# Down weights without row means, output as y times r plus x1, and the last two batches summed by TensorE

## What is computed

```python
x = x + _layernorm(attn(_layernorm(x)))
x = x + _layernorm(ffn(_layernorm(x)))          # the second line is what the change touches
# ffn: xf the tokens, w their weights for the two best of 8 experts
out = _swiglu(xf, sWg, sWu, sWd)                 # shared expert
for e in range(8):
    out = out + w[:, e:e+1] * _swiglu(xf, Wg[e], Wu[e], Wd[e])
# _swiglu(x, wg, wu, wd) = silu(x @ wg) * (x @ wu) @ wd ;  wd is 256x128
# _layernorm(y) = (y - mean(y)) / sqrt(var(y) + 1e-5), over the 128 columns
```

## Time and profile before

| | |
|---|---|
| three runs | 517.92, 518.85, 522.02 us (median 518.85) |
| the profiled execution | 518.35 us, span 516.6 us |
| busy in the span | PE 431.8, PEld 347.9, DVE 340.0, ACT 273.6, POOL 267.4 us |
| chain that ended last | PE 52%, DVE 25%, POOL 6%, issue 6%, DMA 5%, ACT 3% |
| instructions | 9625 |

### The profile page before, as it was taken

The page is one execution under the profiler, slowest core; times in us unless marked ns, Lnnn a source line. Parts: engine busy times, 40 slices in busy tenths (PEclk is TensorE's granted clock), DMA queues, the critical chain, the costliest instruction groups (busy, mean ns, idle before and its releaser), DMA issues.

```text
span 516.6 us, 9625 instructions
## 1 busy us (share of the span) xinstructions
PE 431.8 (84%) x2578; PEld 347.9 (67%) x2578; DVE 340.0 (66%) x1560; ACT 273.6 (53%) x629; POOL 267.4 (52%) x325
## 2 busy tenths in 40 slices
PE   5876989789799999998999999879996799989000
PEld 5645667476687878787878787765895699977000
DVE  7697797977785298539744965564372123199997
ACT  5453565566455574656456643646443254535753
POOL 4000017265475147735772677477777777766400
PEclk9997999999999999999999999999999699999655
DMA  7872001041433323451344225531664767794663
GB/s 235 274 280 82 2 6 59 29 128 58 133 103 113 113 75 97 121 158 60 98 141 134 86 76 153 147 117 60 188 209 138 213 201 204 234 417 148 221 251 122
DMA packets 41562, 73.44 MB, mean 142 GB/s; under 512 B 8771, under 2 KB 23622, under 8 KB 40486
## 3 DMA queue, kind: packets, MB, share of 16 engines
q1 hardware_dynamic: 32870, 54.07, 33.7%
q0 software_dynamic: 8640, 18.76, 10.1%
HBM read 45.41 MB, written 27.39 MB: 141 GB/s over the span
## 4 chain that ended last, share of the span: by engine, by line
PE 52%; DVE 25%; POOL 6%; issue 6%; DMA 5%; ACT 3%; SPq 2%; DVEq 0%; POOLq 0%
PE bank_h L909 7%; PE bank_g L884 7%; PE bank_h L884 6%; POOL slots_dram L655 5%; PE bank_g L892 3%; PE bank_h L892 3%; PE bank_h L919 3%; PE bank_t L813 2%; PE bank_p L884 2%; DMA slots_dram<-u_rows,slot_i 2%; PE bank_p L701 2%; DVE keep L1404 2%; DVE st_r L1290 2%; DVE keep L1886 2%; DVE hid_s L1370 2%
## 5 line engine op out<-in xcount | busy, mean ns | idle before, releaser
L655 POOL DMA_INDIRECT slots_dram<-u_rows,slot_i x128 | 123.2, 963 | 158.7 <-DVE u_rows L1542 122.2
L665 POOL DMA_INDIRECT routed_dram<-pair_rows,yi x142 | 138.3, 974 | 52.7 <-issue 36.1
L1370 DVE TENSOR_TENSOR hid_s<-act_s,bank_h 128x512 f32<-128x512 f32 x68 | 46.4, 682 | 83.7 <-PE bank_h L884 57.3
L884 PE MATMUL bank_h<-xbT,wgu_slots 128*128 128x256 f32 x224 | 59.5, 389 | 8.5 <-DVE hid_s L1370 8.5
L909 PEld LDWEIGHTS bank_h<-wdn,hid_s 128*128 128x128 f32 x408 | 54.1, 194 | 16.6 <-issue 15.0
L1139 ACT ACTIVATE pair_rows<-bank_h,yw 128x128 f32<-128x128 f32 x102 | 31.9, 364 | 62.6 <-PE bank_h L909 62.4
L884 PE MATMUL bank_g<-xbT,wgu_slots 128*128 128x256 f32 x224 | 59.1, 387 | 2.3 <-DMA wgu_slots<-wgu_dram 1.1
L909 PE MATMUL bank_h<-wdn,hid_s 128*128 x408 | 55.2, 279 | 4.0 <-DVE hid_s L1370 2.4
L1051 ACT ACTIVATE act_s<-bank_g 128x512 f32<-128x512 f32 x68 | 40.5, 595 | 26.4 <-PE bank_g L884 14.0
L884 PEld LDWEIGHTS bank_h<-xbT,wgu_slots 128*128 128x128 f32 x224 | 42.1, 192 | 18.2 <-DVE hid_s L1370 12.8
L884 PEld LDWEIGHTS bank_g<-xbT,wgu_slots 128*128 128x128 f32 x224 | 38.7, 193 | 6.8 <-issue 2.2
(11 more groups left out here) (315 smaller groups left out, 934.5 us busy)
## 6 DMA issues: line engine op xcount, KB each, us to landing
wgu_slots<-wgu_dram SPq DMA_DIRECT2D x71, 256.0 KB, 2.6
wgu_slots<-slots_dram SPq DMA_DIRECT2D x36, 144.0 KB, 2.3
xb<-slots_dram SPq DMA_DIRECT2D x35, 144.0 KB, 2.8
keep<-in_L_attn_x SPq DMA_DIRECT2D x8, 512.0 KB, 4.0
work<-routed_dram SPq DMA_DIRECT2D x4, 1024.0 KB, 7.3
out_dram<-keep SPq DMA_DIRECT2D x7, 512.0 KB, 2.6
routed_dram<-pair_rows,yi POOLq DMA_INDIRECT x142, 2.6
wgu_dram<-keep SPq DMA_DIRECT2D x2, 1024.0 KB, 7.6
```

What stands on the lines that cost most here:

```text
L655: g.indirect_dma_start(slots_dram, bass.IndirectOffsetOnAxis(ap=slot_i[k % 2][:, c * NT + t:c * NT + t + 1], axis=0), u_row[k % 2][:, t, : ...
L665: g.indirect_dma_start(routed_dram, bass.IndirectOffsetOnAxis(ap=yi[:, h % (2 * YB), at:at + 1], axis=0), yb[h % YB][:, at, :], None).then ...
L884: last = mm(bank[:, c * W:(c + 1) * W], w_unit(n)[:, which * INTER + c * P:which * INTER + (c + 1) * P], xbT[:, n % RING, :], start=True, ...
L1370: v.tensor_tensor(hid[:, k % RING, :], act_g[k % (RING if k >= PLAIN else 2)], up_bank(k)[:, :], ALU.mult).then_inc(hid_sb, 1)
```

## The change

The mean of a row of `hidden @ wd` over its 128 columns is `hidden` times the row means of `wd`. If each row of every down weight has its mean taken off once, all y have mean zero, and the norm is y*r. So:

- VectorE sums the rows of the shared expert's down weights after step 0 and of the eight experts' after step 1 and scales the sums; GpSimd subtracts them from the weights in place; TensorE waits for that before its first shared and its first expert down product.
- ScalarE adds the attention norm's shift to x1 in place, tile by tile, in stages 2 to 5 of steps 1 to 3 and in slots 5 to 11 of steps 4 to 8.
- The output is one VectorE instruction per tile, x1 = y*r + x1. ScalarE's and VectorE's normalizations and the 1024-wide residual adds go.
- Groups are (0), (1,2), (3,4); batch 5 is summed and measured by VectorE alone; batches 6 and 7 are summed by TensorE: an identity matrix times the shared output and times both rows of each pair, into two PSUM banks per batch. ScalarE squares these tiles with an accumulating output, VectorE makes r from the sums of squares and writes the output straight from PSUM.
- Batch 7 is written and stored lower half first.

```diff
-C_GROUPS = ((0, 1, 8), (1, 2, 8), (3, 2, 8), (5, 2, 6), (7, 1, 4))
+C_GROUPS = ((0, 1), (1, 2), (3, 2))
+X1_TILES = {2: range(0, 2), 3: range(2, 5), 4: range(5, 6), 5: range(6, 8)}
+X1_OF_SLOT = {5: range(0, 2), 6: range(2, 3), 7: range(3, 4), 8: range(4, 5), 9: range(5, 6), 10: range(6, 7), 11: range(7, 8)}
...
+            def centre(blocks, means, count):
+
+                pool.wait_ge(block_means, count)
+                g.tensor_tensor(blocks, blocks, means.unsqueeze(2).to_broadcast(list(blocks.shape)), ALU.subtract).then_inc(centred, 1)
+
+            centre(swdn_blocks, block_mean[:, 0:IC], 1)
+            centre(wdn_blocks, block_mean[:, IC:], 2)
             pool.wait_ge(ew_loaded, 16 * (4 + NE))
...
                 if stage in (4, 6):
+                    if first:
+                        pe.wait_ge(centred, 1)
...
+            pe.wait_ge(centred, 2)
             for s in range(MIX, PLAIN_STEP):
                 mixed(s)
...
+            def sum_routed(b):
+
+                for h in range(2):
+                    mm(sum_banks(b)[h][:, :], ident[:, :], kept(b, (NT + 4 * h) * E, (NT + 4 * h + 4) * E), start=True, stop=False)
+                for h in range(2):
+                    if b == B - 1 and h:
+                        pe.wait_ge(pair_in_2, 16)
+                    else:
+                        pe.wait_ge(pair_in[b % SLOTS_C], 16 * (b // SLOTS_C + 1))
+                    for c in range(2):
+                        last = mm(sum_banks(b)[h][:, :].rearrange("p (t n) -> p t n", n=E), ident[:, :], pair(b)[:, 4 * h:4 * h + 4, c, :], start=False, stop=c == 1)
+                    last.then_inc(tail_ps, 1)
+
+            pe.wait_ge(sy_sb, 2 * B)
+            for b in range(B - 2, B):
+                sum_routed(b)
...
+            def x1_of(k, tiles):
+
+                act.wait_ge(u_dve, k + 1)
+                for t in tiles:
+                    x1 = kept(k, t * E, (t + 1) * E)
+                    ins = A(x1, x1, ACT.Identity, bias=kept(k, 2 * NT * E + t, 2 * NT * E + t + 1))
+                if t == NT - 1:
+                    ins.then_inc(x1_shifted, 1)
...
+            for b in range(B - 2, B):
+                for h in range(2):
+                    act.wait_ge(tail_ps, 2 * (b - (B - 2)) + h + 1)
+                    for t in range(4):
+                        ins = A(squares[b - (B - 2)][:, (4 * h + t) * E:(4 * h + t + 1) * E], sum_banks(b)[h][:, t * E:(t + 1) * E], ACT.Square, accum_out=sq[:, b - (B - 2), 4 * h + t:4 * h + t + 1])
+                ins.then_inc(sq_done, 1)
...
+            def block_means_of(blocks, means):
+
+                wait(inc(v.tensor_reduce(means, blocks, AX.X, ALU.add)))
+                v.tensor_scalar(means, means, 1.0 / E, None, ALU.mult).then_inc(block_means, 1)
+
             for s in range(MIX):
                 for _ in step(s, s % 2):
                     pass
+                if s == 0:
+                    dv.wait_ge(sw_loaded, 16 * 3)
+                    block_means_of(swdn_blocks, block_mean[:, 0:IC])
+                if s == 1:
+                    dv.wait_ge(ew_loaded, 16 * (4 + NE))
+                    block_means_of(wdn_blocks, block_mean[:, IC:])
...
+            def c_out(b, r, y_of, tiles=range(NT)):
+
+                dv.wait_ge(x1_shifted, b + 1)
+                for t in tiles:
+                    x1 = kept(b, t * E, (t + 1) * E)
+                    ins = v.scalar_tensor_tensor(out=x1, in0=y_of(t), scalar=r[:, t:t + 1], in1=x1, op0=ALU.mult, op1=ALU.add)
+                    if t < tiles[-1]:
+                        if t % 2:
+                            yield
+                ins.then_inc(res_ready, 1)
+                yield
...
             def last_stage():
 
...
+                outs = nothing()
+                for g in range(len(C_GROUPS)):
+                    sums = c_sums(*C_GROUPS[g + 1], st_of[(g + 1) % 2]) if g + 1 < len(C_GROUPS) else nothing()
+                    for _ in c_scale(g):
                         next(sums, None)
+                        next(outs, None)
                         yield
+                    for strand in (sums, outs):
                         for _ in strand:
                             yield
+                    outs = c_group_out(g)
                 yield True
+                sums = c_sums(B - 3, 1, st_of[1])
+                for _ in sums:
+                    next(outs, None)
                     yield
+                for _ in outs:
                     yield
+                yield from c_var(ve[:, 0:NT], st_of[1][:, 0:NT, :])
+                dv.wait_ge(sq_done, 1)
+                c = inc(v.tensor_scalar(ve[:, NT:2 * NT], sq[:, 0, :], 1.0 / E, LN_EPS, ALU.mult, ALU.add))
+                wait(c)
+                yield from rsqrt(r_c[:, 1, :], ve[:, :], nt_[:, :])
+                yield from c_out_kept(B - 3, r_c[:, 1, 0:NT])
+                yield from c_out(B - 2, r_c[:, 1, NT:2 * NT], summed(B - 2))
+                dv.wait_ge(sq_done, 2)
+                c = inc(v.tensor_scalar(ve[:, 0:NT], sq[:, 1, :], 1.0 / E, LN_EPS, ALU.mult, ALU.add))
+                wait(c)
+                yield from rsqrt(r_c[:, 0, 0:NT], ve[:, 0:NT], nt_[:, 0:NT])
+                for h in range(2):
+                    yield from c_out(B - 1, r_c[:, 0, :], summed(B - 1), range(h * NT // 2, (h + 1) * NT // 2))
```

More of the change, by code:

```diff
@@ L109 @@
 C_STRAND = 3
-C_NORM_FROM = {0: 68}
-C_NORM_STEP = 2
 PADS_AT = (40, 41, 42, 43)
@@ L580, in _ @@
                 load_pair(b)
-            for b in range(STORED_FIRST):
-                store(b)
             y_landed(UNITS)
             load_last_pair()
-            for b in range(STORED_FIRST, B - 1):
+            for b in range(B - 1):
                 store(b)
@@ L1096, in step @@
                         xn_of(s + 1, 1 - par, XN_TILES[stage])
+                    if has(k) and stage in X1_TILES:
+                        x1_of(k, X1_TILES[stage])
                     if has(k) and stage == EXP_AT:
@@ L1854, in c_scale, with c_var @@
-            def c_scale(g):
-                first, batches, _ = C_GROUPS[g]
-                n_t = batches * NT
-                r, z = r_c[:, g % 2, 0:n_t], shift[:, g % 2, 0:n_t]
-                yield from moments(st_of[g % 2][:, 0:n_t, :], mean_r[:, 0:n_t], sum_r[:, 0:n_t], gap_r[:, 0:n_t], ve[:, 0:n_t], E * LN_EPS, c_last[g % 2])
-                if g >= 2:
-                    dv.wait_ge(y_normed, C_GROUPS[g - 1][0])
-                yield from rsqrt(r, ve[:, 0:n_t], nt_[:, 0:n_t])
-                c = inc(v.scalar_tensor_tensor(out=z, in0=mean_r[:, 0:n_t], scalar=-0.5, in1=r, op0=ALU.mult, op1=ALU.mult))
+            def c_var(var, st):
+                z = NT * (st.shape[1] // NT)
+                sums, gap = sum_r[:, 0:z], gap_r[:, 0:z]
+                wait(c_last[0])
+                inc(v.scalar_tensor_tensor(out=sums, in0=st[:, :, 2], scalar=E * LN_EPS, in1=st[:, :, 5], op0=ALU.add, op1=ALU.add))
+                c = inc(v.tensor_tensor(gap, st[:, :, 1], st[:, :, 4], ALU.subtract))
@@ L1864, in c_scale @@
                 yield
                 wait(c)
[L1866 to L1867 removed]
+                c = inc(v.scalar_tensor_tensor(out=gap, in0=gap, scalar=0.25, in1=gap, op0=ALU.mult, op1=ALU.mult))
                 yield
[L1870 to L1878 removed]
@@ L1880, in c_add, with c_scale @@
-            def c_add(g, k):
-                first, batches, _ = C_GROUPS[g]
+                wait(c)
+                c = inc(v.scalar_tensor_tensor(out=var, in0=sums, scalar=1.0 / E, in1=gap, op0=ALU.mult, op1=ALU.add))
+                yield
+                wait(c)
+            def c_scale(g):
+                n_t = C_GROUPS[g][1] * NT
+                yield from c_var(ve[:, 0:n_t], st_of[g % 2][:, 0:n_t, :])
+                yield from rsqrt(r_c[:, g % 2, 0:n_t], ve[:, 0:n_t], nt_[:, 0:n_t])
```

120 lines of the change are left out of this document (29 added, 91 removed).

## The result

The changed kernel takes 526.84 us (median of 4 runs, 523.94 to 529.08) against 519.47 in the runs of the kernel before beside it: ratio 1.0124, interval 1.0080 to 1.0169. In a later set of runs it was 525.69 against 519.62, ratio 1.0116 (1.0082 to 1.0150). It is slower by some 6 to 7 us, where 518.4 had been forecast and the range ended at 523.5.

A forecast was written before the change was run, and what follows sets the result against it. VectorE was taken to bound the last 61 us and the early steps, TensorE the mixed steps. Span 516.6 - 5.3 + 3.1 + 1.8 = 516.2, plus 1.75 and 0.5, gave 518.4 us; range 513.5 to 523.5.

The forecast's parts named there:

- The last stage: VectorE's list at the end: 22.5 us removed, 17.2 added, so -5.3 us, with bounds of -7.5 and -3.
- the 2.2 us of the working: Batch 0's outputs and two more statistics come before the last hidden product in VectorE's list, delaying it about 2.2 us.
- the third rival: Last stage: batch 7's squares come late and VectorE waits 2 to 4 us, giving 521.4; chance 0.13.
- the late-squares case: Last stage: at 1.2 GHz the four matmuls behind the last load take 8.3 us, squares ready at 504.4; chance 0.13.
- The reduction: VectorE after step 1: summing the experts' weight rows (128x2048) with its scaling costs 2.5 us, hidden by nothing.
- The small reduction's 0.4: VectorE after step 0: reducing 128x256 takes 0.4 us, 0.6 with its scaling, counted in a part of +3.1.
- the front has no slack: Steps 0 to 3: VectorE's turn is not covered, so a microsecond of its work in step 1 moves everything behind it.
- so its own time is hidden: GpSimd's subtraction, 2.9 to 5.9 us for 2048 elements, costs nothing because GpSimd is idle before 74.96, moved to 78.
- The first rival: Step 1's residuals: GpSimd's subtraction blocks VectorE's two-input instructions, about +3.7 us, giving 522.1; chance 0.27.
- The shifts: ScalarE's adding of the shift to x1 costs +1.8 us in all, bounded by 0 and 5.8.
- Slot 11: The last tile's shift, between silu and the router's table load, costs 0.4 us at each boundary behind steps 4 to 7, 1.6 in all.
- In steps 1 to 3 ... VectorE is later still there: 0: Two tiles' shifts delay the query exps by 0.8 us in steps 1 to 3, but cost nothing as VectorE is later.

The follow-up runs named there:

- e1: The changed kernel without the row means of the down weights and without their subtraction: 515.06 us, ratio 0.9913 to the kernel before.
- e2: The changed kernel with ScalarE instead of GpSimd subtracting the row means that VectorE still makes: 520.68 us, ratio 1.0018 to the kernel before.
- e3: The changed kernel with GpSimd's subtraction of the experts' means held back until VectorE's residuals are done: 522.77 us, ratio 1.0059 to the kernel before.
- e9: The changed kernel with 30 matmuls whose results nobody reads ahead of step 2's keys and values: 524.58 us, ratio 1.0085 to the kernel before.
- e4: The changed kernel with the last row tile's shift moved from slot 11 to slot 10 of the mixed steps: 523.86 us, ratio 1.0095 to the kernel before.
- e7: The changed kernel with the shifts of batches 0 to 2 moved from steps 1 to 3 to plain units 40 to 63: 524.49 us, ratio 1.0101.
- e8: The changed kernel's last stage without row means, with only the shifts of batches 0 to 2 in steps 1 to 3: 513.74 us, ratio 0.9880.
- e5: The changed kernel with ScalarE summing and subtracting the means, early shifts in the plain units, the last tile's in slot 10: 514.21 us, ratio 0.9897.
- e6: The changed kernel's last stage alone, row means and shifts left out: 512.31 us, ratio 0.9859 to the kernel before.

## Why the prediction was wrong, point by point

- **The last stage: right.** -5.3 forecast, -5.9 between the two first profiles, -6.4 between the means. 0.26 us for each multiply-add held, for the sixteen from PSUM too (8 in 2.07). The last hidden product came 28.92 us behind the first pair add, not 26.61: the 2.2 us of the working measured 2.3. Batch 7's squares ended 4.6 us before VectorE asked, so the third rival fell. That TensorE's clock was at 1.00 beside the batch 7 sums (3.95 us for four matmuls that the late-squares case put at 8.3) helped.
- **The reduction: right**, 2.4 for 2.5. The small reduction's 0.4 and its scaling's 0.2 were sized right (0.53 in all), and in the changed kernel they do not reach the last hidden product of step 1 (28.33 us against 28.43). That the front has no slack was right for step 1: e1 gave back all of A.
- **The step that failed: "so its own time is hidden", said of GpSimd's subtraction.** GpSimd was idle, but VectorE wasn't. The subtraction took 3.64 us, inside the estimate of 2.9 to 5.9, and VectorE's residuals stood still for 3.36 us of it (5.54 against 2.18, the changed kernel against e2). The first rival had the place, the mechanism and the size (3.7), and was given 0.27. What spoke against it was a GpSimd scatter that lost beside VectorE. That add had started first (452.71, the scatter 452.87), but the order of the starts is not all: in the second profile of the kernel before a scatter began at 478.60 and took 0.96 us, and the add that began at 478.87, inside it, took its usual 1.23. So a scatter did not hold VectorE up where a subtraction did. The Trainium skill (SBUF — State Buffer, section Who interferes with whom) says that a VectorE instruction with two SBUF inputs contends with a GpSimd instruction that reads SBUF and that one with a single SBUF input, outside the two-port modes, doesn't: e3 agrees on both halves, with 1.65 us for eight statistics and 1.91 for one small instruction. Its rule should have outweighed a row on another kind of instruction. The prediction's "no run here shows an element-wise GpSimd instruction beside VectorE" was not quite so: the select at 4.93 ran beside eight statistics of VectorE, which took their usual 1.64 us, the harmless half of that rule.
- **A term that was missing: TensorE's clock when it is made to wait.** The working moved VectorE by microseconds and asked what TensorE waits for, but not at what clock it comes back. In A this is what is left of 7.4 less 2.39 and 3.36: 1.6 us, and 1.7 in e2. e9, which keeps the clock up, gains 0.8, about 1.7 by the estimate above. Even the first rival's 522.1 falls short of 525.7 by this and the next point.
- **Step 8: 1.6 to 3.7 us in D, with no term either.** It goes with the late front (eight profiles of eight, against two of eight), so the change most likely brings it, but by which of its parts is not shown; its price in D, where it comes, is shown.
- **The shifts: sum right in part by luck.** 1.8 forecast, 0.6 + 1.3 measured. Slot 11 was right (e4), with 1.3 for 1.6. "In steps 1 to 3 ... VectorE is later still there: 0" was not: 0.6 (e7, e8).

The sum by the measured pieces: 516.6 - 5.9 + 2.4 + 3.4 + 1.6 + 0.6 + 1.0 + 3.6 = 523.3, against a span of 522.2; the rest is E and the stretch before A, which was 0.8 shorter in this execution.

## What to carry to other kernels

An idle engine is not a free place for work if its instructions hold up the engine on the critical path, as GpSimd's subtraction did here: give such a step to an engine that doesn't (ScalarE in e2 and e5), or lay GpSimd's arithmetic beside VectorE's one-input instructions, as far as these last (e3). Where a change makes TensorE wait longer, reckon with half clock for what it does afterwards, and look at the granted clock of the stretch before trusting a sum of durations. A gain at the end of the list (here 6 us) and a cost at its front (8 us in A and B) of the same change are best measured apart; the kernel that keeps the one and moves the other is then a small step.

## What had not been expected of the hardware

- One GpSimd subtraction of 128x2048 fp32 with a broadcast second operand took 3.64 us and held eight two-input VectorE instructions up by 3.36 us; one of 128x256 took 0.64 us and held eight of them up by 0.35. The Trainium skill (GPSIMD Engine Reference, section 3.1) gives 4.5 us for a two-input add of this size; the measured number is lower here.
- A wait of TensorE of 2.4 us ended at half clock in e2 and e5 and at full clock in e6; one of 5.73 us ended at half clock. In step 8 the same busy time was followed by either clock.
- An activation with an accumulating output shows as two records, 0.28 and 0.20 us, and a run of four of 128 columns goes by at about 0.25 us each: fast enough for ScalarE to square two batches and, in e5, to sum the weights in the gaps of other work.
